# Forming one weight sum by an accumulating DMA in a 7-product FFN kernel, and loading x earlier

## The reference, cut to what matters

```
x = x + xattn(layernorm(x), ctx, ctx, ctx)   # x [8,256,256], ctx [8,120,256]: gelu(x c^T) * (x c^T), times c
n = layernorm(x)
h = silu((n @ w1.T) * s1) * ((n @ w2.T) * s2)        # w1, w2 [1024,256]
h = gelu((h @ h1.T) * t1)                            # h1 [1024,1024]
h = gelu((h @ h2.T) * t2)                            # h2 [1024,1024]
x = x + (h @ w3.T) * s3                              # w3 [256,1024]
```

## Time and profile before

| what | us |
|---|---|
| median of 3 runs (342.0 to 343.48) | 342.24 |
| the profiled execution's own time | 342.24 |
| its span, first to last instruction | 340.4 |
| TensorE busy | 329.5 |
| VectorE busy | 256.4 |
| ScalarE busy | 202.7 |
| GpSimd (POOL) busy | 33.9 |

### The profile page before, as it was taken

The page is one execution under the profiler, slowest core; times in us unless marked ns, Lnnn a source line. Parts: engine busy times, 40 slices in busy tenths (PEclk is TensorE's granted clock), DMA queues, the critical chain, the costliest instruction groups (busy, mean ns, idle before and its releaser), DMA issues.

```text
span 340.4 us, 4764 instructions
## 1 busy us (share of the span) xinstructions
PE 329.5 (97%) x1668; PEld 279.1 (82%) x1668; DVE 256.4 (75%) x476; ACT 202.7 (60%) x334; POOL 33.9 (10%) x65
## 2 busy tenths in 40 slices
PE   7779999999999999999999999999999999999994
PEld 5579888888888888888899888888888888888894
DVE  3567859509966695897779768997988688976684
ACT  2345904275643354867796367669586769576840
POOL 6521025002202100011000000000000000010000
PEclk9999999999999999999999999999999999999998
DMA  5999876991038989434655655536656474443003
GB/s 154 288 376 389 312 235 217 301 393 62 3 110 280 309 301 369 176 123 131 235 168 207 201 182 175 160 141 227 214 190 193 177 272 162 123 126 123 0 13 118
DMA packets 26333, 67.56 MB, mean 198 GB/s; under 512 B 1728, under 2 KB 3136, under 8 KB 24512
## 3 DMA queue, kind: packets, MB, share of 16 engines
q1 hardware_dynamic: 17520, 47.27, 39.6%
q0 software_dynamic: 8784, 19.92, 19.5%
HBM read 56.71 MB, written 10.49 MB: 197 GB/s over the span
## 4 chain that ended last, share of the span: by engine, by line
PE 91%; DMA 5%; POOL 1%; DVE 1%; issue 0%; ACT 0%; SPq 0%; POOLq 0%
PE P L1262 45%; PE P L1325 17%; PE P L1215 15%; PE P L1351 9%; DMA xs<-in_x 3%; DMA W<-in_w 2%; PE P L1163 2%; PE P L1171 2%; PE P L1179 2%; POOL W L487 1%; POOL rs L482 0%; DVE st L793 0%; ACT xt L563 0%; POOL rs L480 0%; DVE st L813 0%
## 5 line engine op out<-in xcount | busy, mean ns | idle before, releaser
L1262 PE MATMUL P<-TR,WR 128*128 128x512 f32 x672 | 152.6, 389 | 0.0
L1262 PEld LDWEIGHTS P<-TR,WR 128*128 128x128 f32 x672 | 126.1, 188 | 26.2
L905 DVE TENSOR_TENSOR TR<-H,TR 128x512 fp32r<-128x512 f32 x84 | 57.4, 688 | 21.0 <-ACT TR L611 18.8
L611 ACT ACTIVATE TR<-H 128x512 fp32r<-128x512 f32 x84 | 52.5, 629 | 22.9 <-DVE H L900 17.3
L1215 PE MATMUL P<-X,W 128*128 128x512 f32 (+1 forms) x320 | 61.4, 349 | 0.1
L1325 PE MATMUL P<-TR,WR 128*128 128x512 f32 x256 | 61.4, 395 | 0.0
L1215 PEld LDWEIGHTS P<-X,W 128*128 128x128 f32 x320 | 51.7, 189 | 8.1 <-DVE X L838 0.5
L1325 PEld LDWEIGHTS P<-TR,WR 128*128 128x128 f32 x256 | 47.7, 188 | 9.7
L601 ACT ACTIVATE SL<-P,sc 128x512 f32<-128x512 f32 (+1 forms) x40 | 24.0, 602 | 27.5 <-PE P L1215 25.4
L878 DVE SCALAR_TENSOR_TENSOR H<-P,sc,SL 128x512 f32<-128x512 f32 (+1 forms) x40 | 25.3, 638 | 15.1 <-ACT SL L601 8.8
L652 ACT ACTIVATE H<-H,sc 128x512 f32<-128x512 f32 x36 | 26.0, 721 | 16.4 <-DVE H L921 16.4
(11 more groups left out here) (70 smaller groups left out, 234.6 us busy)
## 6 DMA issues: line engine op xcount, KB each, us to landing
WR<-in_h POOLq DMA_DIRECT2D x15, 1024.0 KB, 5.4
WR<-blocks_h SPq DMA_DIRECT2D x12, 1024.0 KB, 5.5
H<-in_h SPq DMA_DIRECT2D x8, 1024.0 KB, 10.1
blocks_h<-H SPq DMA_DIRECT2D x8, 1024.0 KB, 7.3
xn<-in_h SPq DMA_DIRECT2D x8, 512.0 KB, 3.7
xt<-in_h SPq DMA_DIRECT2D x8, 512.0 KB, 4.2
W<-in_w POOLq DMA_DIRECT2D x4, 512.0 KB, 6.1
WR<-in_w POOLq DMA_DIRECT2D x2, 1024.0 KB, 5.5
```

Source lines behind the costliest of these rows:

```text
L611: eng.activation(TR[:, f % RING, 0, :], operand(c, L, s, kk), ACT.Copy).then_inc(s_hi, 1)
L905: eng.tensor_tensor(TR[:, f % RING, 1, :], operand(c, L, s, kk), TR[:, f % RING, 0, :].bitcast(f32), ALU.subtract).then_inc(s_lo, 1)
L1262: out_ = eng.matmul(bank(c, L, s, m)[:, :], WR[r % WRING][:, at:at + 128], TR[:, f % RING, h, :], start=(s in FRESH and kk == 0 and h == 0 ...
```

## The change

Two things are changed.

First, the weights of product 1 are no longer stored as a sum and loaded from it. `load_both` on the POOL queue loads block 2 into the ring buffer, waits until it has landed (`s_acc`), and then loads block 3 onto it with a DMA that adds to its destination (`accum_op`). `sums_out` stores three of the four combined blocks, 768 KB and not 1024 KB. The three `load_sum` of product 1 are gone from the SP queue, and `sums_out(6)` stands ahead of the first two `load_check`.

Second, the SP queue no longer waits for W12 before x tiles 2 and 3, which are issued before the column scales `sc`. On the POOL queue `rstd(0, 1, 1)` stands after the first of the four loads of W12, and not after the last.

```diff
-STORED = {2: 0, 3: 1, 4: 2, 1: 3}
+STORED = {2: 0, 3: 1, 4: 2}
...
-                eng.dma_start(dst, raw(q)).then_inc(s_S[q], 16)
+                eng.dma_start(dst, raw(q)[:, 0:3, :]).then_inc(s_S[q], 16)
...
-            eng.dma_start(sc[:, :], cols).then_inc(s_sc, 16)
-
-            for i in range(4):
-                eng.wait_ge(s_w12[i], 16)
             load_x(2)
             load_x(3)
+            eng.dma_start(sc[:, :], cols).then_inc(s_sc, 16)
             load_cf(1)
...
             sums_out(5)
+            sums_out(6)
             load_check(0)
             load_check(1)
-            sums_out(6)
-            load_sum(0, 1, 1)
             load_sum(0, 1, 2)
...
-            load_sum(1, 0, 1)
...
-            load_sum(1, 1, 1)
...
+            def load_both(c, L):
+                r = entry(c, L, 1)
+                w = (h1, h2)[L]
+                to = place(r).rearrange("p (k o) -> p k o", k=4)
+                reuse(eng, r - WRING)
+                eng.dma_start(to, w[:, :, 2, :]).then_inc(s_acc, 16)
+                eng.wait_ge(s_acc, 16 * (layer_no(c, L) + 1))
+                eng.dma_start(to, w[:, :, 3, :], accum_op=ALU.add).then_inc(s_v[r % WRING], 16)
...
             def load_layer(c, L):
                 load_w(c, L, 0)
+                load_both(c, L)
                 load_w(c, L, 5)
...
-            for i in range(4):
+            load_w12(0)
+            rstd(0, 1, 1)
+            for i in range(1, 4):
                 load_w12(i)
-            rstd(0, 1, 1)
...
             rstds(13, (1, 6), (1, 7))
+            load_both(0, 1)
             load_w(0, 1, 5)
```

More of the change, by code:

```diff
@@ L124, in xattn_ffn @@
         s_S = [sem(f"s_S{i}") for i in range(8)]
+        s_acc = sem("s_acc")
         s_w = [sem(f"s_w{i}") for i in range(WRING)]
@@ L406, in _ @@
             load_sum(0, 1, 4)
-            load_check(3)
-            load_check(4)
-            load_sum(1, 0, 1)
-            load_check(5)
+            for i in range(3, 6):
+                load_check(i)
             for q in range(4):
@@ L422, in _ @@
             load_sum(1, 0, 4)
-            for i in range(16, 20):
+            for i in range(16, TESTS):
                 load_check(i)
-            load_sum(1, 1, 1)
-            load_check(20)
-            load_check(21)
-            for p in (2, 3, 4):
+            for p in STORED:
                 load_sum(1, 1, p)
```

## The result

The changed kernel took 356.86 us (median of 4 runs, 355.94 to 358.4); the kernel before, on the same chip, 342.12 (341.19 to 343.48). The ratio is 1.0432, with a 95% interval of 1.0379 to 1.0485: slower by 14.7 us, where 4.2 were forecast. The profiled execution has a span of 354.5 us against 340.4, 14.1 more.

A forecast was written before the change was run, and what follows sets the result against it. TensorE bounds the kernel from about 29 us on; before, DMAs and VectorE lead the chain. 342.24 + 0.2 (start) + 3.0 (layer (0, 1)) + 0 (layer (1, 0)) + 1.0 (layer (1, 1)) = 346.4 us, range 341.0 to 353.0.

The forecast's parts named there:

- the three places where it put a cost: The start, net +0.2 us; product 1 of layer (0, 1), +3.0; product 1 of layer (1, 1), +1.0.
- x tiles 2 and 3 earlier, -1.8: At the start: x tile 2 lands near 8 us, not 22.9, so VectorE's wait goes, a gain of 1.8 us.
- W12 under the traffic let loose, +2.0: At the start: W12's last load lands at 18.0 us beside the SP queue, TensorE needs it near 16.0: +2.0 us.
- my upper end, 20.2: Slow case for W12: 2.1 MB at 196 GB/s from 9.5 us end at 20.2, a loss of 4.2 us.
- The net of the start: x tile gain and W12 loss together: -1.8 + 2.0 = +0.2 us, between -1.8 and +2.4.
- The price of an add, 8.1 quiet: An adding 1 MB load takes 8.1 us in a quiet stretch, between 5.4 and 10.8.
- Layer (0, 1), +3.0: Product 1: the add, beside the SP queue, lands at 133.9 us against a need at 130.9: +3.0 us.
- the upper end of 6.8: Product 1 of layer (0, 1): the add lands as late as 137.7 us, a stall of 6.8 us.
- Product 2 behind sums_out(7), covered: Layer (0, 1): the store may come 1 to 4 us later; cover is 5.0 us with product 1 late, so no cost.
- Layer (1, 1), +1.0, and layer (1, 0), 0: Product 1: in (1, 1) the add lands at 277.6 us against 276.8, +1.0; in (1, 0) 52 us cover two loads.
- The third: Rival, much slower: the add costs two contended loads and W12 gets half rate; 354.9 us, chance 0.13.
- The third end, +3.5 in layer (1, 1): Product 1 of layer (1, 1): an add of 10.8 us and 1 us of contention, +3.5 us.

The follow-up runs named there:

- start-only kernel: The kernel before with only the queue edits at the start (x tiles early, no wait for W12, `rstd` after the first W12 load): 346.37 us, ratio 1.0125.
- the kernel with SP held: The changed kernel with the SP queue held ahead of `sums_out(6)` until the added weights of layer (0, 1) have landed: 356.45 us, ratio 1.0439.

## Why the prediction was wrong

The direction was right, and so were two of the three places where it put a cost; the size was wrong, and 356.86 lies outside 341 to 353. The forecast was +4.2 and the trace has +14.2. The 10 us between them are +4.0 at the start, +4.5 for the stall in layer (0, 1), +2.5 for the clock behind it and -1.0 in layer (1, 1). Step by step:

**x tiles 2 and 3 earlier, -1.8.** Right, as shown by the kernel that does only this.

**W12 under the traffic let loose, +2.0.** This term was mis-sized. W12's last load landed at 20.06 and TensorE's second group began at 20.20, where the prediction put it at 16.0: a loss of 4.2. I had halved it, in part on the ground that the first load of the earlier trace rows lost nothing. That load had a head start of 1.4 us on a SP queue that had been idle; W12 met a full one. Between its first landing (5.72 + 8.3 = 14.0) and its last, W12 moved 1.57 MB in 6.0 us, 260 GB/s, two thirds of the 382 to 399 that went in all. It lost its full speed but kept the larger share against a queue of mostly 2 KB runs. So my upper end, 20.2, was met by luck: it came from 196 GB/s from 9.5 on, and what came about was a higher rate behind a first load that landed 3.2 us late (14.0, before 10.8). The prediction had let the data begin at 9.5 as before. Then the clock, at 0.50 until 22.9, cost another 1.9 us (20.20 to 28.93 is 8.73 us, and 6.79 with the clock up; in the start-only kernel, where it was 1.4, the clock was back sooner, at 0.90 in 22.9 to 25.0 and not at 0.64), which took back the 1.9 that the earlier x tile gave. The net of the start is +4.2 in the trace (3.7 by the medians of the start alone), not +0.2.

The Trainium skill ("DMA: Bandwidth & Descriptors", section "Queues, rings and completion order") has the engines take turns packet by packet. For W12, in runs of 4 KB, that gives two thirds, and the trace agrees; for the second load of layer (0, 1) the runs here do not: longer packets helped by much less than it gives.

**The price of an add, 8.1 quiet.** Right: 8.2 in the kernel with SP held, 8.2 in layer (1, 1) of the changed kernel. The statement of the Trainium skill ("Collectives: The Full Stack", section "The bandwidth ceiling: the fold count and why AG ≠ RS ≠ AR") that an add costs a second source read fits the 185 GB/s at a full DMA share.

**Layer (0, 1), +3.0.** This is the step that failed most. I summed the bytes of both queues from 120.4, let them drain at 334 GB/s to 137.7, and put the add in the middle of that. It landed at 142.5, which is 138.3 on the prediction's scale, where all stood 4.2 us earlier: after the end, not in the middle. Two things were wrong. The bytes do not bound the add: the SP queue was refilled at 135 with the set for product 3 and the next test load, 1.57 MB that my sum left out, so the add was contended to its end. What counts is the share that it gets meanwhile: 1.05 MB less in the queue changed nothing, longer runs changed a little. And 334 GB/s did not hold, since an add takes a full DMA share for 185 GB/s; the stretch moved 281 and 302. The stall was 7.5 us, past the upper end of 6.8. The refill in the changed kernel's SP queue:

```profile
135.07 0.32 SPq L347 DMA_DIRECT2D WR<-blocks_h  x1
135.44 0.49 SPq L356 DMA_DIRECT2D xn<-in_w  x1
```

**The fall of the clock, absent from the sum.** The prediction read a clock of 1.00 over an idle time of 1.92 us and said that a gap costs only its own length. That was true of that gap. It did not carry over to idle times of 2.6 and 7.5 us, behind which the clock was 0.50: 1.9 us at the start, counted above, and +2.5 in layer (0, 1), shown by the kernel that fills the stall. Neither the sum nor a rival had either.

**Product 2 behind sums_out(7), covered.** The store landed at 128.28 + 14.5 = 142.8, or 138.6 on the prediction's scale, and not at 134.2: 4.4 us later, past the 1 to 4 allowed. The stall covered it: ScalarE's snap began at 142.88 and TensorE had only then started product 1.

**Layer (1, 1), +1.0, and layer (1, 0), 0.** The adds landed at 282.33 + 8.2 = 290.5 and the slot was at 233.01 + 8 x 7.254 = 291.0: no wait, where +1.0 was forecast. The add was issued 5.8 us after the buffer was free, where I had 6.2, and it took 8.2 us although a test load and the next set went out beside its second half (from 286.79): the microsecond that I put on for them was not there.

**The rivals.** The third, all at their ends, gave 354.9 and had 0.13. Two of its three ends, the start and layer (0, 1), were passed, and they were not independent: both are a POOL load beside a full SP queue, so it should have had more. The third end, +3.5 in layer (1, 1), did not come at all. That its total comes so near is in part luck: against it the trace has +1.8 at the start, +0.7 for the stall, +2.5 for the clock and -3.5 in layer (1, 1), together +1.5, and the median lies 0.5 above the profiled execution.

## What to carry to other kernels

A load that must be on time beside another busy queue is priced by the share that it gets there, for as long as the other queue is not empty, and not by the bytes that stand in line; what sets that share was not settled here. Of two serial loads for one buffer the second starts late, here in the full stretch (5.1 us for the first, 13.4 for a plain second), and an add moved its data at about half the rate of a plain load (185 against 380 GB/s). A stall of TensorE is priced with the slow stretch behind it. A wait that holds back transfers nobody needs yet may be what keeps the needed one fast: move the one tile that is late ahead of it, and leave the wait.

## What was not expected of the hardware

- A plain 1 MB load in 2 KB runs took 5.1 us with little beside it and 13.4 beside a full SP queue; in 8 KB rows, in the same place, 10.9.
- An add of 1 MB took 8.2 us alone, 9.0 and 10.1 in layer (1, 0) beside other traffic and 15.9 to 16.3 beside a full queue, and moved 185 GB/s at a full DMA share.
- TensorE idle for 1.9 us kept a granted clock of 1.00. Behind 2.3 us (the plain load in 8 KB rows) the six products still took 45.4 us and not 43.5. Idle for 7.5 us it had 0.50 for about 4 us afterwards, and with 64 small matmuls in the idle time it kept 1.00.
